# Skewed sums of a delay correlation: both skews read on alternate partitions, halves added by VectorE, one product a tile

## Chip, cores, metric

One NeuronCore of a Trainium2 chip. The time is the device time of one execution in microseconds. Most runs of a kernel agree within 0.3%.

## What is computed

Two layers on x (2 batches, 2048 tokens, width 512): an attention by delays, then a mixture of experts. Only the first matters here:

```python
q, k, v = layernorm(x) @ Wq + bq, ctx @ Wk + bk, ctx @ Wv + bv   # ctx: 128 tokens, padded to L = 2048
qf, kf = rfft(q over time), rfft(k over time)
corr = irfft(qf.real * kf.real + 1j * -(qf.imag * kf.imag), n=L)  # mean over heads and channels
weights, delay = top_k(mean(corr), 15)                            # per batch
out = sum_i softmax(weights)_i * roll(v, delay_i)
x = x + out @ Wo + bo
x = x + shared_expert(layernorm(x)) + routed_experts(layernorm(x))   # 16 experts, 4 a token
```

## The kernel before

Tokens lie in 8 blocks of 512 rows (4 of batch 0, then 4 of batch 1), each of 4 tiles of 128. The engines run hand-written streams that meet by semaphores; each engine's order is the program's.

The kernel needs no FFT. correlate(q) (L704) makes P^T, the product of 128 context rows with a block of 512 normalised tokens, into PSUM, and ScalarE's save_pt (L1163) stores it in `pt[b]`, 128 rows by 2048 columns with 128 columns of wrap-around on either side. The correlation at a delay is a sum over P^T's diagonals. The even part and the odd part of the formula need the sums in both directions. So SyncE writes pt to DRAM (`pt_dram`) and reads it back twice, each row moved by one column more (pitch PTW + 1, `skew_d`) or one less (pitch PTW - 1, `skew_c`): then a diagonal is a column, over 128 partitions. skewed_sum(b, a) (L716) sums the columns of tile a (128 columns, NA = 16 tiles) on TensorE: two products with 32 columns of constants each, of which the last two count: skew_c by (1, 1) and skew_d by (1, -1), which leaves the sum and the difference of the two directions. 16 tiles and 2 batches make 32 sums and 64 products. All are f32, which takes two passes a product.

Batch 0, up to 56 us. skew_early(0) and (1) (columns 0 to 1023, 1024 to 1535) and skew_late(0) (the rest and the wrap) are issued by SyncE as save_pt makes their columns. TensorE weaves the sums into the projections of batch 1's correlation (second_g) and of the values (value_part), L837 to L856. Then come VectorE's save_sums, TensorE's even_parts (three products), VectorE's save_even, TensorE's mean_correlation (17 products), and on VectorE save_mean, best_of_tiles, best_of_all, tile_weights with small DMAs between them, which leave the 15 delays and their weights. SyncE writes these to DRAM and reads them as a circulant tile `st`, with which attention(0) starts. In VectorE's stream moments(6) stands between save_even(0) and save_mean(0). invert_total, x1_tile(0, 0 to 3), x1_moments(0), normalise(7), second_normalise(0), the low halves, x1_tile(1, 0) and vo_low(1) follow attention's start. TensorE waits for vo_low(1) (L896) before it turns the rows of block 0.

GpSimd in this stretch: add_bo(q) adds the output bias to block q of x, four adds of 128 x 512. Five blocks are added from 31 us on, the others after the circulant tile is in and the first weights of the shared expert have been issued. It also issues batch 1's early skewed copies (L2027, L2028), the late ones being SyncE's, and waits for the late ones before it overwrites a buffer beside them.

Batch 1, 100 to 120 us. The shared expert runs in chunks of 128 hidden columns: shared_half(g, half) makes 12 products of 512 columns for gate (half 0) and for up (half 1), ScalarE makes silu(g), VectorE the product, shared_down(g) follows a chunk later. half 0 of chunk g + 1 waits for silu(g) (L996). SUM_AT (L85) says behind which product a sum of batch 1 stands: ten in chunk 0, six in chunk 1. After them even_parts(1) and, behind shared_down(0), mean_correlation(1). logits(1) (L1033) of the router comes at the end of chunk 2, and waits for block 1's turned rows: VectorE normalises, ScalarE and GpSimd split into halves (GpSimd's second_norm_lo, behind its wait for the late skewed copies), SyncE writes them and reads them transposed.

From 130 us on nothing is touched: chunks 2 to 36, 143 blocks of routed experts, the last chunks of the shared expert.

## Time and profile before

| | us |
|---|---|
| median of 3 runs | 997.05 |
| lowest, highest | 996.57, 1002.86 |
| profiled execution | 997.35 |
| its span | 995.5 |

Busy in the span: TensorE 983.8, weight loads (beside the products) 601.3, VectorE 649.9, GpSimd 478.1, ScalarE 380.4. The granted clock of TensorE is at full speed throughout. In a timeline a line is a run of like instructions: start, time from the start of the first to the end of the last, count, and in brackets how long the engine was idle before it and what ended that. Ends of pipelined products overlap the next start, so the time of one is read from start to start. Engines: PE TensorE, DVE VectorE, ACT ScalarE, POOL GpSimd, SPq SyncE's queue.

### The profile page before, as it was taken

How to read it: one execution, taken by the hardware profiler on the slowest of the kernel's cores; microseconds unless marked ns; L12 is line 12 of the kernel's file. 1: busy time of each engine (PE TensorE's matmuls, PEld its weight loads, DVE VectorE, ACT ScalarE, POOL GpSimd, SP SyncE). 2: the span in 40 equal slices, each digit the busy share in tenths (PEclk: the TensorE clock that was granted, in tenths of full speed). 3: DMA queues.
4: the chain of work that ended last, by engine and by line, in shares of the span. 5: the costliest groups of instructions: out<-in, count | busy, mean ns of one | idle time of the engine just before them, and what ended most of it. 6: DMA issues, size and time to landing. Idle time of an engine off the chain costs nothing.

```text
span 995.5 us, 21034 instructions
## 1 busy us (share of the span) xinstructions
PE 983.8 (99%) x6750; PEld 601.3 (60%) x6750; DVE 649.9 (65%) x1506; ACT 380.4 (38%) x776; POOL 478.1 (48%) x540
## 2 busy tenths in 40 slices
PE   8999999999999999999999999999999999999998
PEld 7776644444444445557777777777777544444443
DVE  4977788874488898765555555555455375676765
ACT  3646454443445333324444444444444311111111
POOL 0725412131144577754445444454543376766662
PEclk9999999999999999999999999999999999999999
DMA  9735867868562721558889988889988579999675
GB/s 340 266 126 194 293 196 233 232 184 240 180 180 96 220 66 58 133 140 255 251 240 245 257 236 253 238 252 234 253 253 224 171 237 271 310 259 304 193 225 177
DMA packets 175484, 216.93 MB, mean 218 GB/s; under 512 B 101097, under 2 KB 112233, under 8 KB 174377
## 3 DMA queue, kind: packets, MB, share of 16 engines
q1 hardware_dynamic: 151640, 136.95, 46.6%
q0 software_dynamic: 23760, 78.79, 26.7%
q8 instruction: 61, 1.00, 0.4%
q14 instruction: 23, 0.18, 0.1%
HBM read 123.67 MB, written 69.22 MB: 194 GB/s over the span
## 4 chain that ended last, share of the span: by engine, by line
PE 84%; DVE 7%; DMA 4%; issue 2%; SPq 1%; ACT 1%; POOL 1%; another core or an unknown queue 0%; DVEq 0%; POOLq 0%; ACTq 0%
PE bank L1068 18%; PE bank L941 14%; PE bank L1131 14%; PE bank L1092 9%; PE bank L957 7%; PE bank L1144 7%; PE bank L1051 5%; PE bank L716 2%; PE bank L1082 2%; PE bank L793 1%; DMA arena<-in_x 1%; PE bank L696 1%; SPq L517 1%; PE bank L706 1%; DMA pt_dram<-arena 1%
## 5 line engine op out<-in xcount | busy, mean ns | idle before, releaser
L1068 PE MATMUL bank<-arena 128*128 x1716 | 211.1, 273 | 0.9 <-DVE arena L1608 0.9
L941 PE MATMUL bank<-arena 128*128 128x512 f16 x888 | 202.3, 379 | 0.5 <-DVE arena L1616 0.2
L1068 PEld LDWEIGHTS bank<-arena 128*128 128x128 f16 x1716 | 163.0, 98 | 26.5 <-issue 1.9
L2139 POOL DMA_INDIRECT arena<-y_dram,arena x128 | 137.0, 1071 | 76.8 <-issue 34.2
L2082 POOL DMA_INDIRECT arena<-xr_dram,arena x143 | 139.7, 977 | 58.4 <-issue 47.0
L941 PEld LDWEIGHTS bank<-arena 128*128 128x128 f16 x888 | 87.2, 99 | 101.0 <-DVE arena L1616 0.7
L1131 PE MATMUL bank<-arena 128*128 128x512 f16 x648 | 144.1, 379 | 0.0
L1092 PE MATMUL bank<-arena 128*128 x429 | 115.4, 378 | 0.8 <-ACT arena L1401 0.5
L1884 DVE SCALAR_TENSOR_TENSOR arena<-bank,arena 128x128 f32<-128x128 f32 x143 | 41.7, 292 | 109.7 <-ACT arena L1390 83.6
L1951 DVE SCALAR_TENSOR_TENSOR arena<-arena 128x512 f32<-128x512 f32 x128 | 95.4, 749 | 25.4 <-DMA arena<-y_dram,arena 19.8
L1131 PEld LDWEIGHTS bank<-arena 128*128 128x128 f16 x648 | 63.4, 98 | 76.5
L1338 ACT ACTIVATE arena<-arena 128x512 f16<-128x512 f32 x64 | 40.3, 629 | 171.7 <-DVE arena L1616 94.2
L957 PE MATMUL bank<-arena 128*128 128x512 f16 x444 | 101.9, 379 | 0.3 <-DVE arena L1622 0.3
L1390 ACT ACTIVATE arena<-bank 128x128 f32<-128x128 f32 x143 | 39.7, 278 | 144.4 <-PE bank L1068 92.0
L2075 POOL COPY arena<-arena 128x1 int32 (+1 forms) x143 | 28.1, 197 | 118.9 <-PE bank L1051 109.5
L1401 ACT ACTIVATE arena<-bank 128x512 f32<-128x512 f32 x143 | 83.2, 582 | 1.9 <-PE bank L1092 1.4
L1887 DVE TENSOR_TENSOR arena<-arena 128x128 f16<-128x128 f32 x143 | 41.9, 293 | 53.6 <-ACT arena L1394 49.1
L1608 DVE COPY arena<-bank 128x1024 f16<-128x1024 f16 x108 | 73.7, 682 | 2.9 <-PE bank L1051 1.6
L957 PEld LDWEIGHTS bank<-arena 128*128 128x128 f16 x444 | 43.3, 98 | 52.4 <-DVE arena L1622 0.8
L1144 PE MATMUL bank<-arena 128*128 128x512 f16 x324 | 74.2, 379 | 0.0
L1051 PEld LDWEIGHTS bank<-arena 128*128 128x128 f16 x864 | 57.1, 97 | 26.0 <-DMA arena<-xr_dram,arena 0.9
L2048 POOL TENSOR_TENSOR arena<-arena 128x1024 f32 (+1 forms) x16 | 34.5, 2155 | 69.8 <-ACT arena L1347 58.5
(227 smaller groups left out, 1313.4 us busy)
## 6 DMA issues: line engine op xcount, KB each, us to landing
y_dram<-arena SPq DMA_DIRECT2D x143, 256.0 KB
arena<-in_x SPq DMA_DIRECT2D x8, 1024.0 KB, 12.5
xr_dram<-arena SPq DMA_DIRECT2D x16, 512.0 KB, 4.0
x_dram<-arena SPq DMA_DIRECT2D x8, 1024.0 KB, 5.8
arena<-in_gu_w SPq DMA_DIRECT2D x16, 512.0 KB, 3.5
out<-arena SPq DMA_DIRECT2D x32, 256.0 KB
arena<-x_dram SPq DMA_DIRECT2D x5, 1024.0 KB, 5.9
arena<-in_gu_w POOLq DMA_DIRECT2D x8, 512.0 KB, 4.8
```

Of the source, the lines that this page charges most:

```text
L941: last = mm(bank[half][:, :], (gu_hi_s, gu_lo_s)[wp][:, c, at:at + H], xt[:, xv * KC + kc, :], start=(n == 0), stop=(n == 3 * KC - 1))
L957: last = mm(bank[2 + t][:, :], s_hb[:, g % 2, hv, t * P:t * P + P], (dn_hi_s, dn_lo_s)[wp][:, c, :], start=(c == 0 and n == 0), stop=((c = ...
L1051: last = turn(bank16[p % 2][:, n * P:n * P + P], xg[:, s % 4, n * P:n * P + P], id16)
L1068: last = mm(gate_up_bank(s, s)[:, 0:2 * H], rows[:, xv * KC + kc, :], only((gu_hi_r, gu_lo_r)[wp], e, slice(kc * 2 * H, (kc + 1) * 2 * H)) ...
L1092: last = mm(bank[6 + j][:, :], r_hT[:, j, hv, :], only((dn_hi_r, dn_lo_r)[wp], e), start=(n == 0), stop=(n == 2))
L1131: last = mm(bank[GATE_UP[n % 2][g]][:, :], (gu_hi_s, gu_lo_s)[wp][:, c, at:at + H], xt[:, xv * KC + kc, :], start=(m == 0), stop=(m == 3 * ...
L1144: last = mm(bank[2 + t][:, :], s_hb[:, n % 2, hv, t * P:t * P + P], (dn_hi_s, dn_lo_s)[wp][:, c, :], start=(first and m == 0), stop=(c == ...
L1401: A(y_sb[n % 4], bank[6 + n % 2][:, :], ACT.Copy, scale=1.0 / WS).then_inc(s_ye, 1)
L1608: V.tensor_copy(xgT[:, j, :, :], bank16[j].rearrange("p (n q) -> p n q", n=2 * KC)).then_inc(s_txe, 1)
L1951: V.scalar_tensor_tensor(acc, ybuf[n % RING][:, e, :], w, acc, ALU.mult, ALU.add).then_inc(s_cmb, 1)
L2082: pool.indirect_dma_start(out=dst, out_offset=None, in_=xr_dram[:, :], in_offset=bass.IndirectOffsetOnAxis(ap=token_now[:, r:r + 1], axis= ...
L2139: pool.indirect_dma_start(out=ybuf[n % RING][:, e, :], out_offset=None, in_=y_dram[:, :], in_offset=bass.IndirectOffsetOnAxis(ap=row_of[:, ...
```

## The change

- The two skews are read into one buffer: the one of pitch PTW - 1 on even partitions, the one of pitch PTW + 1 on odd ones. Each partition gets two rows of P^T, r and r + 64, the one in `skew_near`, the other in `skew_far`. In batch 0 one DMA of 64 partitions x 2 rows writes both; in batch 1, where the two buffers are far apart, each copy is two DMAs (GpSimd issues four for two, SyncE six for three).
- VectorE adds far to near (fold_part): columns 128 to 895, 896 to 1407, then (fold_late) 0 to 127 and 1408 to 2047 for batch 0; 128 to 1407, then the rest, for batch 1. `s_fold` counts them, and TensorE waits for it where it waited for the copies.
- A sum is one product, by ones and by +1 on even, -1 on odd partitions.
- TensorE's order for batch 0: second_g(1) without sums, turn_first(4), four sums in each of second_g(2) and (3), value_part(0), the wait for fold 3, the last six sums, value_part(1), even_parts, value_part(2), mean_correlation, value_part(3).
- Batch 1: all 16 sums in chunk 1; fold_part(1) follows x1_moments(1), fold_late(1) stands in VectorE's chunk 0 between the product h and its low half.
- VectorE's splits of the router's weights and its small conversions move from before normalise(5) to behind vo_low(0).
- GpSimd adds three blocks at first, waits until the even parts are saved, adds block 3 and half of block 4, and the other half after the first weights.

Cut to its changed lines:

```diff
@@ -82,8 +82,9 @@
 PACE = (3, 5)
-SUM_AT = {(0, 0, 10): 1, (0, 0, 11): 2, **{(0, 1, n): i + 3 for i, n in enumerate((0, 1, 3, 4, 6, 7, 9, 10))},
-          (1, 0, 11): 0, **{(1, 1, n): n + 11 for n in range(NA - 11)}}
+SUM_AT = {**{(1, 0, n): n + 1 for n in range(10)}, (1, 0, 10): 0, (1, 0, 11): 11,
+          **{(1, 1, n): n + 12 for n in range(NA - 12)}}
+FOLD = P // 2
 WEIGHTS = {1: (3, 4), 2: (5,), 4: (6,), 5: (7,)}
...
@@ -104,7 +105,8 @@
     c[:, C_ID:C_ID + P] = eye
-    c[:, C_ONES:C_ONES + 4] = [1, 1, 1, -1]
+    c[:, C_ONES:C_ONES + 4] = 1
+    c[1::2, C_ONES + 3] = -1
     c[0, C_J0] = 1
...
@@ -174,8 +176,9 @@
         xnT = [view(o + 64 * KB, [KC, BLK]), view(o + 72 * KB, [KC, BLK])]
-        skew_c = [view(o + 80 * KB, [L]), view(o + 88 * KB, [L])]
-        skew_d = [view(o + 88 * KB, [L]), view(24 * KB, [L])]
+        skew_near = [view(o + 80 * KB, [L]), view(o + 88 * KB, [L])]
+        skew_far = [view(o + 88 * KB, [L]), view(24 * KB, [L])]
+        skew_both = view(o + 80 * KB, [2, L])
         xtb_c = view(o + 80 * KB, [2, 2 * KC, BLK], F16)
...
@@ -319,7 +322,11 @@
-            return bass.AP(pt_dram, b * P * PTW + start + first, [[pitch, P], [1, end - first]])
+            return bass.AP(pt_dram, b * P * PTW + start + first, [[pitch, FOLD], [FOLD * pitch, 2], [1, end - first]])
+        def skewed_half(b, start, pitch, first, end, v):
+            return bass.AP(pt_dram, b * P * PTW + start + v * FOLD * pitch + first, [[pitch, FOLD], [1, end - first]])
...
@@ -334,6 +341,7 @@
         s_sk, s_sk2 = ([sem(f"skew_{part}_in{b}") for b in range(B)] for part in ("early", "late"))
+        s_fold = sem("skew_folded")
         s_u, s_u_sb = sem("sums_done"), sem("sums_saved")
...
@@ -460,9 +468,9 @@
                 sp.wait_ge(s_ptw[0], 16 * (n + 1))
-                sp.dma_start(skew_c[0][:, max(lo - M, 0):hi - M], skewed(0, 2 * M - 1, PTW - 1, max(lo - M, 0), hi - M)
-                             ).then_inc(s_sk[0], 16)
-                sp.dma_start(skew_d[0][:, max(lo, M):hi], skewed(0, 1, PTW + 1, max(lo, M), hi)).then_inc(s_sk[0], 16)
+                sp.dma_start(skew_both[0:P:2, :, max(lo - M, 0):hi - M],
+                             skewed(0, 2 * M - 1, PTW - 1, max(lo - M, 0), hi - M)).then_inc(s_sk[0], 16)
+                sp.dma_start(skew_both[1:P:2, :, max(lo, M):hi], skewed(0, 1, PTW + 1, max(lo, M), hi)).then_inc(s_sk[0], 16)
...
@@ -470,9 +478,17 @@
                 sp.wait_ge(s_ptw[b], 16 * (2 if b else len(STEPS[0]) + 2))
-                sp.dma_start(skew_c[b][:, EARLY - M:L], skewed(b, 2 * M - 1, PTW - 1, EARLY - M, L)).then_inc(s_sk2[b], 16)
-                sp.dma_start(skew_d[b][:, EARLY:L], skewed(b, 1, PTW + 1, EARLY, L)).then_inc(s_sk2[b], 16)
-                sp.dma_start(skew_d[b][:, 0:M], skewed(b, 1, PTW + 1, 0, M)).then_inc(s_sk2[b], 16)
+                if b == 0:
+                    sp.dma_start(skew_both[0:P:2, :, EARLY - M:L], skewed(0, 2 * M - 1, PTW - 1, EARLY - M, L)
+                                 ).then_inc(s_sk2[0], 16)
+                    sp.dma_start(skew_both[1:P:2, :, EARLY:L], skewed(0, 1, PTW + 1, EARLY, L)).then_inc(s_sk2[0], 16)
+                    sp.dma_start(skew_both[1:P:2, :, 0:M], skewed(0, 1, PTW + 1, 0, M)).then_inc(s_sk2[0], 16)
+                else:
+                    for v, dst in enumerate((skew_near[1], skew_far[1])):
+                        sp.dma_start(dst[0:P:2, EARLY - M:L], skewed_half(1, 2 * M - 1, PTW - 1, EARLY - M, L, v)
+                                     ).then_inc(s_sk2[1], 16)
+                        sp.dma_start(dst[1:P:2, EARLY:L], skewed_half(1, 1, PTW + 1, EARLY, L, v)).then_inc(s_sk2[1], 16)
+                        sp.dma_start(dst[1:P:2, 0:M], skewed_half(1, 1, PTW + 1, 0, M, v)).then_inc(s_sk2[1], 16)
...
@@ -726,27 +742,20 @@
                 dst = SUMS[b][:, SUM_W * a:SUM_W * a + SUM_W]
-                mm(dst, skew_c[b][:, a * P:a * P + P], c_sb[:, C_ONES + 2 - SUM_W:C_ONES + 2], start=True, stop=False)
-                return mm(dst, skew_d[b][:, a * P:a * P + P], c_sb[:, C_ONES + 4 - SUM_W:C_ONES + 4], start=False, stop=True)
+                return mm(dst, skew_near[b][:, a * P:a * P + P], c_sb[:, C_ONES + 4 - SUM_W:C_ONES + 4],
+                          start=True, stop=True)
...
                     last = mm(dst, lhs(k), rhs(k), start=(k == 0), stop=(k == KC - 1))
-                    if k < len(tiles):
-                        summed = skewed_sum(0, tiles[k])
+                    skewed_sum(0, tiles[k])
                 last.then_inc(s_mm, 1)
-                return summed
...
                                 lambda k: column(kT, k, 1), tiles)
-            def value_part_and_sum(c, tiles):
-                return project_and_sum(bank[5][:, c * M:c * M + M], lambda k: wv_sb[:, k, c * P:c * P + P],
-                                       lambda k: column(ctx_sb, k, 0), tiles)
...
@@ -836,29 +845,30 @@
             second_g(0)
-            pe.wait_ge(s_sk[0], 32)
-            second_g_and_sum(1, (1, 2))
-            skewed_sum(0, 3)
+            second_g(1)
             turn_first(4)
-            for a in (4, 5, 6):
+            pe.wait_ge(s_fold, 1)
+            second_g_and_sum(2, (1, 2, 3, 4))
+            for a in (5, 6):
                 skewed_sum(0, a)
-            pe.wait_ge(s_sk[0], 64)
-            second_g_and_sum(2, (7, 8))
-            second_g_and_sum(3, (9, 10))
+            pe.wait_ge(s_fold, 2)
+            second_g_and_sum(3, (7, 8, 9, 10))
...
             pe.wait_ge(s_pt_sb, 4)
-            pe.wait_ge(s_sk2[0], 48)
-            value_part_and_sum(0, (0, 11, 12))
-            summed = value_part_and_sum(1, (13, 14, 15))
+            value_part(0, bank[5], 0)
+            pe.wait_ge(s_fold, 3)
+            for a in (0, *range(11, NA)):
+                summed = skewed_sum(0, a)
             summed.then_inc(s_u, 1)
-            value_part(0, bank[5], 2)
+            value_part(0, bank[5], 1)
             pe.wait_ge(s_tables, 32)
...
             even_parts(0)
+            value_part(0, bank[5], 2)
+            mean_correlation(0)
             value_part(0, bank[5], 3)
-            mean_correlation(0)
             pe.wait_ge(s_mm_sb, 18)
...
@@ -933,11 +943,11 @@
                     at = kc * 2 * H + half * H
-                    if g == half == 0 and n == 10:
-                        pe.wait_ge(s_sk[1], 32)
+                    if g == 1 and half == 0 and n == 0:
+                        pe.wait_ge(s_fold, 4)
                         pe.wait_ge(s_pt_sb, 7)
-                    if g == 1 and half == 0 and n == 11:
-                        pe.wait_ge(s_sk2[1], 48)
+                    if g == 1 and half == 0 and n == 10:
+                        pe.wait_ge(s_fold, 5)
                     last = mm(bank[half][:, :], (gu_hi_s, gu_lo_s)[wp][:, c, at:at + H], xt[:, xv * KC + kc, :],
...
@@ -1429,6 +1439,17 @@
+            def fold_part(b, lo, hi):
+                near = skew_near[b][:, lo:hi]
+                return V.tensor_tensor(near, near, skew_far[b][:, lo:hi], ALU.add)
+            def fold_late(b):
+                dve.wait_ge(s_sk2[b], 96 if b else 48)
+                fold_part(b, 0, M)
+                fold_part(b, EARLY - M, L).then_inc(s_fold, 1)
             def save_sums(b):
...
@@ -1534,20 +1555,12 @@
             normalise(4)
-            dve.wait_ge(s_misc, 64)
-            dve.wait_ge(s_const, 16)
-            r3 = rt32.rearrange("p (k e) -> p k e", k=KC)
-            link.done(V.tensor_scalar(rt_hi, r3, WS, None, ALU.mult))
-            V.scalar_tensor_tensor(rt_lo, r3, WS, rt_hi, ALU.mult, ALU.subtract).then_inc(s_rt, 1)
-            V.tensor_copy(id16, c_sb[:, C_ID:C_ID + P]).then_inc(s_rt, 1)
-            V.tensor_copy(tri16, cr_sb[:, R_TRI:R_TRI + P])
-            V.memset(chosen_after[:, 0:E], 0.0)
-            V.tensor_copy(places16, cr_sb[:, R_BLK:R_BLK + COLUMNS])
+            for n, (lo, hi) in enumerate(STEPS[0]):
+                dve.wait_ge(s_sk[0], 32 * (n + 1))
+                fold_part(0, max(lo, M) if n == 0 else lo - M, hi - M).then_inc(s_fold, 1)
             V.memset(ones_row[0:1, :], 1.0)
-            dve.wait_ge(s_ids, 1)
-            V.tensor_scalar(token_id, token_int, -ID_MID, None, ALU.add)
-            V.memset(ones16, 1.0).then_inc(s_rt, 1)
             normalise(5)
+            fold_late(0)
             save_sums(0)
...
@@ -1559,6 +1572,18 @@
             vo_low(0)
+            dve.wait_ge(s_misc, 64)
+            dve.wait_ge(s_const, 16)
+            r3 = rt32.rearrange("p (k e) -> p k e", k=KC)
+            link.done(V.tensor_scalar(rt_hi, r3, WS, None, ALU.mult))
+            V.scalar_tensor_tensor(rt_lo, r3, WS, rt_hi, ALU.mult, ALU.subtract).then_inc(s_rt, 1)
+            V.tensor_copy(id16, c_sb[:, C_ID:C_ID + P]).then_inc(s_rt, 1)
+            V.tensor_copy(tri16, cr_sb[:, R_TRI:R_TRI + P])
+            V.memset(chosen_after[:, 0:E], 0.0)
+            V.tensor_copy(places16, cr_sb[:, R_BLK:R_BLK + COLUMNS])
+            dve.wait_ge(s_ids, 1)
+            V.tensor_scalar(token_id, token_int, -ID_MID, None, ALU.add)
+            V.memset(ones16, 1.0).then_inc(s_rt, 1)
...
@@ -1618,6 +1643,8 @@
                     x1_tile(ATTEND[g], 2, 6)
+                if g == 0:
+                    fold_late(1)
                 dve.wait_ge(s_shh, g + 1)
...
@@ -1668,6 +1695,8 @@
             x1_moments(1)
+            dve.wait_ge(s_sk[1], 64)
+            fold_part(1, M, EARLY - M).then_inc(s_fold, 1)
             shared_weights_lo(1)
...
@@ -1992,11 +2021,11 @@
-            def add_bo(q):
+            def add_bo(q, tiles=range(TB)):
...
                 pool.wait_ge(s_xna, 2 * (q + 1))
-                for t in range(TB):
+                for t in tiles:
                     xq = x_sb[:, q * TB + t, :]
...
@@ -2012,27 +2041,33 @@
             pool.wait_ge(s_xn, 2 * 4)
-            for q in range(5):
+            for q in range(HALF - 1):
                 add_bo(q)
+            pool.wait_ge(s_ev_sb, 3)
+            add_bo(3)
+            add_bo(4, (0, 1))
             pool.wait_ge(s_mm, 18)
...
                 shared_weights_in(n)
+            add_bo(4, (2, 3))
             add_bo(5)
...
             pool.wait_ge(s_mm, 28)
-            pool.dma_start(skew_c[1][:, 0:EARLY - M], skewed(1, 2 * M - 1, PTW - 1, 0, EARLY - M)).then_inc(s_sk[1], 16)
-            pool.dma_start(skew_d[1][:, M:EARLY], skewed(1, 1, PTW + 1, M, EARLY)).then_inc(s_sk[1], 16)
+            for v, dst in enumerate((skew_near[1], skew_far[1])):
+                pool.dma_start(dst[0:P:2, 0:EARLY - M], skewed_half(1, 2 * M - 1, PTW - 1, 0, EARLY - M, v)
+                               ).then_inc(s_sk[1], 16)
+                pool.dma_start(dst[1:P:2, M:EARLY], skewed_half(1, 1, PTW + 1, M, EARLY, v)).then_inc(s_sk[1], 16)
             pool.wait_ge(s_wlo, 1)
...
             pool.wait_ge(s_pt, NB)
-            pool.wait_ge(s_sk2[1], 48)
+            pool.wait_ge(s_sk2[1], 96)
             for n in range(4, 6):
...
```

## Rows read from the trace of the kernel before

**Rows 1.** The page's busy line: us, share of the span, instructions.

```profile
PE 983.8 (99%) x6750; PEld 601.3 (60%) x6750; DVE 649.9 (65%) x1506; ACT 380.4 (38%) x776; POOL 478.1 (48%) x540
```

**Rows 2.** Waits of TensorE: us in total, times, longest.

```profile
PE bank L923 <- DMA arena<-xr_dram: 0.3, 1, 0.3
```

**Rows 3.** TensorE's timeline, 47 to 111 us: start us, us, line, [idle before].

```profile
47.12 0.39 PE L729 MATMUL bank<-arena 128*128 128x32 f32 x2
47.34 0.39 PE L730 MATMUL bank<-arena 128*128 128x32 f32 x2
...
56.13 1.06 PE L696 MATMUL bank<-arena 128*128 128x128 f32 x8
...
58.91 3.66 PE L781 MATMUL bank<-arena 128*16 128x128 f32 x32
...
77.59 2.75 PE L793 MATMUL bank<-arena 128*128 128x512 f16 x12 [0.52 <-DMA arena<-g_dram]
...
93.66 0.61 PE L905 MATMUL bank<-arena 128*128 128x128 f16 x8
...
103.03 0.30 PE L729 MATMUL bank<-arena 128*128 128x32 f32 x2
103.17 0.39 PE L730 MATMUL bank<-arena 128*128 128x32 f32 x2
103.39 0.38 PE L941 MATMUL bank<-arena 128*128 128x512 f16 x1
...
110.93 2.75 PE L941 MATMUL bank<-arena 128*128 128x512 f16 x12
```

**Rows 4.** VectorE's timeline, 40 to 93 us.

```profile
40.66 2.97 DVE L1527 TENSOR_SCALAR arena<-arena 128x512 f32<-128x512 f32 x2
...
58.07 2.46 DVE L1509 BATCH_NORM_STATS2 arena<-arena 128x6 f32<-128x512 f32 x4
...
62.61 0.28 DVE L1449 COPY arena<-bank 16x128 f32<-16x128 f32 x1 [1.45 <-PE bank L781]
...
72.48 1.00 DVE L1527 TENSOR_SCALAR arena<-arena 128x512 f32<-128x512 f32 x2
...
78.51 0.75 DVE L1569 SCALAR_TENSOR_TENSOR arena<-bank,arena 128x512 f32<-128x512 f32 x1 [4.35 <-issue]
...
88.62 2.49 DVE L1659 TENSOR_TENSOR arena<-arena 128x512 f16<-128x512 f32 x4
...
92.49 0.67 DVE L1499 TENSOR_TENSOR arena<-bank,arena 128x512 f16<-128x512 f32 x1
```

**Rows 5.** VectorE's timeline, 300 to 308 us, the first beside GpSimd's work.

```profile
300.46 2.50 DVE L1796 TENSOR_TENSOR arena<-arena 128x512 f32<-128x512 f16 x1
...
307.18 0.69 DVE L1796 TENSOR_TENSOR arena<-arena 128x512 f32<-128x512 f16 x1
```

**Rows 6.** GpSimd's timeline, its adds to x.

```profile
30.85 25.31 POOL L2001 TENSOR_TENSOR arena<-arena 128x512 f32<-128x512 f32 x20 [29.87 <-DVE arena L1527]
...
80.46 4.98 POOL L2001 TENSOR_TENSOR arena<-arena 128x512 f32<-128x512 f32 x4
...
96.12 0.56 POOL L2027 DMA_DIRECT2D arena<-pt_dram  x1
```

**Rows 7.** SyncE's queue, two issues at 47 us.

```profile
46.96 0.43 SPq L475 DMA_DIRECT2D arena<-pt_dram  x1
47.43 0.43 SPq L436 DMA_DIRECT2D arena<-in_x  x1
```

**Rows 8.** These two DMAs: KB each, us to landing.

```profile
arena<-pt_dram SPq DMA_DIRECT2D x1, 64.0 KB, 3.3
...
arena<-in_x SPq DMA_DIRECT2D x1, 1024.0 KB, 8.1
```

**Rows 9.** ScalarE's timeline, the first silu.

```profile
109.63 0.60 ACT L1332 ACTIVATE arena<-bank 128x512 f32<-128x512 f32 x1
```

**Rows 10.** Chain that ended last, 76 to 137 us.

```profile
107.72 4.92 DMA arena<-pt_dram
```

## The prediction

> **What bounds the kernel now.** I read the page's busy lines first: TensorE works 983.8 of 995.5 us and every other engine at most two thirds of the span [rows 1]. So time can only be won by taking work from TensorE, and it stays won only if TensorE finds its next inputs ready. Next the waits of TensorE: they are short, and two of them stand in the stretch that the change touches [rows 2, 3]. At 77.59 us it waited 0.5 us for the first circulant tile, the end of the chain mean correlation, best delays, weights, DMA; at 135.8 us it waited 0.3 us for turned rows of block 1. A chain that already ends 0.5 us after TensorE arrives is not shortened by shortening TensorE's filling work; it moves only as far as its own start moves. Last the timeline of each engine from 40 to 136 us, for who would be late once TensorE comes earlier.
>
> **The products removed.** A skewed sum is two f32 products, each in two passes. Back to back one product takes 47.34 - 47.12 = 0.22 us; between the 512-column products of the shared expert a sum takes 103.39 - 103.03 = 0.36 us, of which the first product 0.14 and the second 0.22 [rows 3]. In both places the removed product is worth 0.22 us, so 32 of them are worth 7.1 us, 3.6 us in each batch. This is 0.7% of the time; the two waits could add 0.8 us to it. No more than 8 us can be gained.
>
> **The additions, batch 0.** VectorE adds 128 x 2048 elements in four instructions. A tensor_tensor over 512 columns is 2.49 / 4 = 0.62 us [rows 4], so 768, 512 and 128 + 640 columns are about 0.95, 0.68 and 1.0 us. GpSimd's adds are the disturbance: a VectorE pair that takes 1.00 us alone took 2.97 us beside them, and a tensor_tensor of 0.69 us took 2.50 us [rows 4, 5]. By these rows a VectorE instruction waits until GpSimd's current one (25.31 / 20 = 1.27 us [rows 6]) is over. By the Trainium skill, SBUF — State Buffer, section "Who interferes with whom", a VectorE instruction with two SBUF inputs or in a two-port mode and a GpSimd one exclude each other for a whole instruction; the trace agrees, with the 2.97 us beside 1.00.
>
> GpSimd now stops after 12 adds, at 30.85 + 12 x 1.27 = 46.1 us [rows 6]. The first addition starts when VectorE is through with its pair at 43.5 us [rows 4], waits about 1 us and ends near 45.5 us, when TensorE has its second turned projection and transposes behind it: no wait. The second ends near 46.7 us, before it is asked for. The router's conversions, moved behind VectorE's last work before attention, lie in its idle time there: about 1.4 us in the 4.35 us for which it was idle before its first addition to x at 78.51 us [rows 4]; 1.4 is an estimate, 0.2 us for each of seven small instructions.
>
> The late part is the first that is late. Its last copy is issued at 46.96 us and lands 3.3 us later [rows 7, 8], at 50.3; the addition makes it 51.3 us. When is TensorE there? Before, all sums of batch 0 were done at 56.13 us [rows 3]. Take off 16 x 0.22 = 3.57 us, and what now stands behind the wait: six sums of 0.22 and one value part of 0.9 us (the one at 56.13 us gives way to the even parts 0.9 us later). That is 50.3 us, so TensorE waits about 1.0 us. Bounds: 0 if the copy comes a microsecond early, 2.5 if the new shape of copy costs 1.5 us more.
>
> **The chain to attention.** Before, the mean correlation ended at 58.91 + 3.66 = 62.6 us [rows 3]. Now: 62.6 - 3.57 + 1.0 - 0.9 (one value part placed behind it) = 59.1. But VectorE has moments(6) in front of saving the mean. That block of x is issued at 47.43 and lands 8.1 us later, at 55.5 us [rows 7, 8], so moments(6), which by TensorE's pace could start at 58.07 - 3.57 + 1.0 - 0.9 = 54.6 (the even parts now stand ahead of one more value part), starts at 55.6. It takes 3.1 us (from 58.07 to 61.16, where the idle 1.45 us before 62.61 begins), and its last instruction, a small tensor_scalar, now meets GpSimd's six adds, which begin after the even parts are saved: up to 1 us more, by the pair above; I take 0.8. The mean is saved near 59.5 instead of 62.61 us [rows 4], 3.1 us earlier. From there the chain took 77.59 - 62.61 = 15.0 us; I add 0.5 us, half way between no meeting with GpSimd and one. Attention starts near 75.0 us, 2.6 us earlier. TensorE itself, with the moved value part behind the mean, would be there at 74.5.
>
> **GpSimd's remaining adds.** At 80.46 us GpSimd made four adds in 4.98 us [rows 6]; now it makes six there, 2.5 us more. Counted from the start of attention these fall on VectorE's normalisation of block 7, two tensor_scalars that cost 1.5 instead of 0.5 us each under it, and on two small ones ahead of them: about 2.2 us of delay. VectorE is busy without a gap from there to vo_low(1), which ended at 92.49 + 0.67 = 93.16 us, and TensorE passes the wait for it at 93.66 us [rows 3, 4]. The slack is 0.5 us, so TensorE now waits 2.2 - 0.5 = 1.7 us, taken as 1.6. Bounds: 0 (the VectorE work hides between adds) and 2.5 (all of the GpSimd time). The gain left here is 2.6 - 1.6 = 1.0 us.
>
> **Batch 1.** Chunk 0 loses ten sums of 0.36 us, so TensorE comes to chunk 1 at 110.93 - 3.6 = 107.3 us in the old clock [rows 3]. It may start it only when ScalarE's silu(0) is done, at 109.63 + 0.60 = 110.2 us [rows 9]. ScalarE is not faster; its chain (weights by DMA, conversion, table load, silu) gets 0.3 to 0.5 us longer, because GpSimd issues four copies of 0.56 us instead of two ahead of the weights [rows 6]. So TensorE waits about 3.3 us. In chunk 1 it then makes 16 sums of one product (16 x 0.14 = 2.3 us) where before it made six of two (6 x 0.36 = 2.2 us). Sum: -3.6 + 3.3 + 0.1 = -0.2 us, taken as -0.3. Bounds: -3.5 if silu(0) moves up with TensorE, +1.5 if the weights land as much later as the two more issues last. The 3.6 us of batch 1 are lost almost whole. The late copies of batch 1 are six instead of three, 0.43 us of issue each [rows 7]. Their last landed at 107.72 + 4.92 = 112.6 us [rows 10]; three issues more make it 113.9, less what the writes ahead of them gain, since they now go out before the weights rather than behind them (up to 1.5 us). With 1.0 us for the addition VectorE is done near 114.5; TensorE asks at 110.7 + 10 x 0.36 = 114.3. No wait of size. The rows of block 1 come 0.5 us earlier or later than before; that wait of 0.3 us stays between 0 and 1.
>
> **Sum.** Against the profiled execution's 997.35 us (span 995.5): attention 2.6 earlier, GpSimd's adds -1.6, batch 1 0.3 earlier: 2.6 - 1.6 + 0.3 = 1.3 us earlier in all. 997.35 - 1.3 = 996.05, forecast 996.0. The median of the runs shown, 997.05, is 0.3 us under the profiled one; that is within what runs differ.
>
> **The rivals.**
> - *The gain stays.* If silu(0) and vo_low(1) are no walls because VectorE and ScalarE move up with TensorE, the 7.1 us come through: 990. For it: most of their work is released by TensorE. Against: the idle of ScalarE before silu(0) is a table load and a DMA, and VectorE has no gap before vo_low(1). With one of the two walls only: 992 to 993.
> - *Slower: copies on alternate partitions are slow.* Each now writes 64 partitions two apart. If that doubles their roughly 3 us, the late part of batch 0 lands 2 to 3 us later, TensorE's 1.0 us wait becomes 3 to 4, and batch 1's late part (4.92 us) takes up to 4 more, on the way to chunk 1's tiles and to the rows of block 1: 996 + 2.5 + 4 = 1002.5. It ends above the old time from 1.3 us of extra landing, both batches together. For it: no row has such a pattern. Against: bytes, run lengths and number of runs are the old ones. By the Trainium skill, SBUF — State Buffer, section "Door 1: The DMA port swizzle", the port follows from higher bits of the partition number, so that alternate partitions still reach all of them and nothing is lost; no row here can show it.
> - *Slower by the lock.* If each VectorE instruction of the chain after the mean meets GpSimd, five or so of 1 us, attention does not come earlier: 996 + 2.6 + 1 = 999.5.
> - *The change saves less than it counts.* If a lone product costs 0.22 and not 0.14 between 512-column products, batch 1 costs 16 x 0.08 = 1.3 us more: 997.3.
>
> **How the numbers follow.** Forecast (994 to 998.5, with the last rival in it) 0.60; the gain stays in one or both places (989 to 994) 0.20; slower by the lock (998.5 to 1001) 0.11; slow copies (over 1001) 0.09. The range leaves out some 0.1 on each side: 990.5 to 1001. What a measurement can tell from no change is about 1%, 10 us: faster would need more than the 8 us that there are, 0.02; slower by over 10 us needs slow copies at worse than half rate, 0.04.
>
> **What would show it.** In the profile after: 32 products of 0.22 us gone; TensorE's waits near 50 us (for the addition, 1.0), near 92 us (for VectorE, 1.6) and before chunk 1 (for ScalarE's silu, 3.3); attention starting near 75.0 us; VectorE's normalisation of block 7 at about 1.5 us an instruction. I am wrong if TensorE shows no wait before chunk 1, if the copies land later than 3.3 us after issue, or if attention starts before 74 or after 76.5 us.

## The result, and the profile after

Before 996.57 us (995.94 to 1002.86, 5 runs), after 1007.65 us (1007.05 to 1009.13, 5 runs): ratio 1.0103, 95% interval 1.0084 to 1.0123. The prediction was 996.0, range 990.5 to 1001: the kernel is slower by 1.0%, and the time lies outside the range. The profiled execution took 1009.13 us, 1.5 us more than the median; its span is 1007.3 us, against 995.5 us. Each experiment below has its ratio, with a 95% interval, to the kernel before as it ran beside it on the same chip. There the median of the kernel before lay between 996.98 and 998.99 us, so experiments are compared by their ratios and stages, not by their times.

The page's busy line, where [rows 1] stood for before. The 32 products are gone, at two records each (6750 to 6686), yet TensorE is busy 2.0 us longer:

```profile
PE 985.8 (98%) x6686; PEld 600.9 (60%) x6686; DVE 655.0 (65%) x1513; ACT 380.7 (38%) x776; POOL 475.9 (47%) x542
```

Waits of TensorE after (line, what ended them, us in total, times, longest). Before, the wait for the block's rows was [rows 2], and none stood at the sums:

```profile
PE bank L745 <- DVE arena L1445: 3.9, 1, 3.9
PE bank L802 <- DVE arena L1674: 2.7, 1, 2.7
PE bank L1061 <- DMA arena<-xr_dram,arena: 2.1, 1, 2.1
PE bank L915 <- DVE arena L1520: 1.8, 1, 1.8
```

TensorE's timeline after, answering to [rows 3] (L745 sums, L712 value parts, L780 even parts, L790 mean, L802 attention, also its products woven into the shared expert, L915 turned rows, L951 shared_half):

```profile
49.29 1.14 PE L712 MATMUL bank<-arena 128*128 128x128 f32 x8
54.28 2.77 PE L745 MATMUL bank<-arena 128*128 128x32 f32 x12 [3.85 <-DVE arena L1445]
56.86 2.06 PE L712 MATMUL bank<-arena 128*128 128x128 f32 x8
58.71 0.47 PE L780 MATMUL bank<-arena 128*128 128x32 f32 x2
...
62.24 4.61 PE L790 MATMUL bank<-arena 128*16 128x128 f32 x32
...
82.08 2.75 PE L802 MATMUL bank<-arena 128*128 128x512 f16 x12
...
100.07 0.61 PE L915 MATMUL bank<-arena 128*128 128x128 f16 x8 [1.76 <-DVE arena L1520]
...
116.02 1.46 PE L802 MATMUL bank<-arena 128*128 128x512 f16 x3 [2.66 <-DVE arena L1674]
118.52 0.61 PE L951 MATMUL bank<-arena 128*128 128x512 f16 x1 [1.03 <-ACT arena L1342]
```

A value part takes 2.06 us instead of 1.06, the mean 4.61 instead of 3.66 [rows 3]. The busy time by stretches after says why (the columns are the length of the stretch, the busy time of TensorE, weight loads, VectorE, ScalarE and GpSimd, then the granted clock, DMA share, GB/s):

```profile
50.00:52.00 2.00, 0.43 (x4) 0.24 (x3) 0.00 (x0) 0.13 (x1) 0.00 (x0) 1.00 0.81 201
52.00:54.00 2.00, 0.00 (x0) 0.00 (x0) 0.80 (x2) 0.00 (x0) 0.00 (x0) 0.98 1.06 398
54.00:64.00 10.00, 9.72 (x45) 8.86 (x46) 4.44 (x16) 0.00 (x0) 3.51 (x3) 0.50 0.58 214
...
116.00:122.00 6.00, 4.94 (x19) 3.32 (x20) 5.24 (x10) 4.98 (x7) 1.08 (x2) 0.50 0.87 279
```

The granted clock was 1.00 (2.4 GHz) until the wait, and 0.50 (1.2 GHz) for the 10 us behind it; the same again from 116 us, behind the wait before chunk 1. Where the copies went, in SyncE's queue after ([rows 7, 8] before), first the three late copies as issued, then their landings, then the first addition in VectorE's timeline:

```profile
46.93 0.59 SPq L482 DMA_DIRECT2D arena<-pt_dram  x1
47.56 0.61 SPq L484 DMA_DIRECT2D arena<-pt_dram  x1
48.22 0.61 SPq L485 DMA_DIRECT2D arena<-pt_dram  x1
```

```profile
arena<-pt_dram SPq DMA_DIRECT2D x1, 320.0 KB, 3.3
arena<-pt_dram SPq DMA_DIRECT2D x1, 256.0 KB, 3.2
arena<-pt_dram SPq DMA_DIRECT2D x1, 64.0 KB, 5.0
```

```profile
53.20 1.03 DVE L1445 TENSOR_TENSOR arena<-arena 128x128 f32<-128x128 f32 x2 [5.05 <-DMA arena<-pt_dram]
```

The last copy is issued 1.3 us later than before and takes 5.0 instead of 3.3 us: 53.2 instead of 50.3 us, and the addition starts at that moment. TensorE came to its wait at 54.28 - 3.85 = 50.43 us.

Start of the stages in each profiled execution, us (late sums: TensorE's last six sums of batch 0; mean: its mean correlation; attention, turned rows: of block 0; even(1): the even parts of batch 1; entry: the first turned rows of the routed experts; the rest is the span behind it):

| kernel | late sums | mean | attention | turned rows | chunk 0 | even(1) | entry | rest |
|---|---|---|---|---|---|---|---|---|
| before | with the value parts | 58.91 | 77.59 | 93.66 | 100.64 | 119.19 | 430.14 | 565.4 |
| after | 54.28 | 62.24 | 82.08 | 100.07 | 107.23 | 128.38 | 439.18 | 568.1 |
| a1_plain_copies | 50.84 | 54.96 | 73.93 | 92.05 | 99.21 | 120.87 | 431.18 | 567.7 |
| a2_keep_clock | 54.60 | 58.82 | 77.71 | 95.75 | 102.90 | 124.12 | 435.33 | 573.3 |
| a3_batch0_only | 53.23 | 61.19 | 80.97 | 98.92 | 106.08 | 125.83 | 436.48 | 567.5 |
| a4_batch1_only | as in before | 59.06 | 77.80 | 93.86 | 100.85 | 120.89 | 431.65 | 568.0 |
| b1_halves | 54.73 | 62.68 | 82.09 | 100.04 | 107.20 | 130.33 | 440.85 | 566.8 |
| b2_no_pause | 54.25 | 62.20 | 81.39 | 97.46 | 104.44 | 126.21 | 436.71 | 569.3 |
| b3_fill | 53.01 | 56.55 | 77.12 | 95.22 | 102.39 | 124.63 | 435.48 | 567.3 |
| b4_silu_first | as in before | 58.47 | 77.36 | 93.42 | 100.41 | 127.76 | 438.01 | 569.1 |
| c1_batch0_filled | 54.37 | 58.73 | 79.53 | 95.60 | 102.59 | 121.59 | 431.85 | 564.7 |
| c2_before_again | as in before | 58.88 | 77.64 | 93.70 | 100.69 | 120.31 | 431.07 | 564.8 |
| c3_batch1_clock | as in before | 58.54 | 77.29 | 93.35 | 100.34 | 122.53 | 432.80 | 564.7 |
| d1_batch0_covered | 56.27 | 60.39 | 79.49 | 95.56 | 102.54 | 122.03 | 433.05 | 564.9 |

Of the 11.8 us of span lost, 4.5 are there at attention, 1.9 more at the turned rows, 2.8 more at even(1), and 2.8 behind the entry. How much one trace can be trusted is seen from before and c2_before_again, which are the same kernel: they differ by 1.1 us at even(1), where only the second waits 1.15 us for batch 1's early copies, and by 0.9 us at the entry. A difference of about 1 us between two single traces is therefore not shown to come from an edit.

### The profile page after: what moved, and what is told of

Same layout as the page of the kernel before. It is cut to its first block, busy times and chain, and to the rows that moved or that the text cites. A ratio compares the mean times of both kernels' runs of the same rounds, so it can differ in the third digit from the quotient of the medians.

```text
span 1007.3 us, 20919 instructions
## 1 busy us (share of the span) xinstructions
PE 985.8 (98%) x6686; PEld 600.9 (60%) x6686; DVE 655.0 (65%) x1513; ACT 380.7 (38%) x776; POOL 475.9 (47%) x542
## 4 chain that ended last, share of the span: by engine, by line
PE 80%; DVE 9%; DMA 5%; issue 3%; SPq 2%; ACT 1%; POOL 1%; DVEq 0%; POOLq 0%; ACTq 0%
PE bank L1078 18%; PE bank L1141 14%; PE bank L951 13%; PE bank L1102 9%; PE bank L967 7%; PE bank L1154 6%; PE bank L1061 5%; PE bank L732 2%; PE bank L1092 2%; DMA pt_dram<-arena 1%; DMA arena<-in_x 1%; DVE arena L1884 1%; DMA arena<-pt_dram 1%; SPq L533 1%; PE bank L802 1%
## 5 line engine op out<-in xcount | busy, mean ns | idle before, releaser
L951 PE MATMUL bank<-arena 128*128 128x512 f16 x888 | 203.3, 380 | 1.7 <-ACT arena L1342 1.0
L951 PEld LDWEIGHTS bank<-arena 128*128 128x128 f16 x888 | 88.0, 100 | 103.3 <-ACT arena L1342 1.9
L1061 PE MATMUL bank<-arena 128*128 128x128 f16 x864 | 66.2, 219 | 2.9 <-DMA arena<-xr_dram,arena 2.1
```

The source lines that it names most:

```text
L951: last = mm(bank[half][:, :], (gu_hi_s, gu_lo_s)[wp][:, c, at:at + H], xt[:, xv * KC + kc, :], start=(n == 0), stop=(n == 3 * KC - 1))
L1061: last = turn(bank16[p % 2][:, n * P:n * P + P], xg[:, s % 4, n * P:n * P + P], id16)
```

## The experiments

**The form of the copies.** a1_plain_copies keeps all else of after, but copies as before (all 128 partitions, one row each); it leaves out the split into even and odd partitions that the constants count on, so its sums are not the right ones:

```diff
-sp.dma_start(skew_both[0:P:2, :, EARLY - M:L], skewed(...))   # pitch PTW - 1
-sp.dma_start(skew_both[1:P:2, :, EARLY:L], skewed(...))       # pitch PTW + 1
+sp.dma_start(skew_near[b][:, EARLY - M:L], skewed_all(...))   # and so for all copies
+sp.dma_start(skew_far[b][:, EARLY:L], skewed_all(...))
```

> The changed kernel with its skewed copies in the old form: each skew read by one DMA into all 128 partitions, one row each, in both batches and from both issuing engines. VectorE still adds two buffers, TensorE still makes one product a tile (the sums are then not those of the reference). Theory 'copies': the new form is what comes late (issues of 0.60 us for 0.43, the last late copy landing at 53.2 for 50.3 us), so here the last addition of batch 0 ends near 51.5 us, TensorE waits about 1 us before it instead of 3.9, its clock stays at full speed from 54 to 64 us, attention starts near 76 us instead of 82, the time is 1000 to 1002. Theory 'order': the wait comes from TensorE being early and from the additions, whatever the copies; then it stays at 3 us or more, the clock falls, and the time stays within 2 us of 1007.65.

Measured: 1001.29 us, ratio 1.0018 (0.9996 to 1.0039). The last late copy in its SyncE queue:

```profile
46.58 0.43 SPq L487 DMA_DIRECT2D arena<-pt_dram  x1
```

It landed after 3.0 us. TensorE's timeline and clock of a1_plain_copies:

```profile
50.84 1.42 PE L741 MATMUL bank<-arena 128*128 128x32 f32 x12
...
110.30 0.61 PE L947 MATMUL bank<-arena 128*128 128x512 f16 x1 [3.20 <-ACT arena L1338]
```

```profile
50.00:66.00 16.00, 16.00 (x112) 12.61 (x112) 11.57 (x37) 6.24 (x19) 7.40 (x6) 1.00 0.51 188
106.00:110.00 4.00, 0.82 (x3) 0.21 (x3) 3.91 (x8) 3.22 (x4) 1.09 (x2) 0.83 0.55 159
110.00:115.00 5.00, 4.70 (x21) 4.08 (x22) 2.99 (x7) 2.67 (x4) 1.41 (x3) 0.50 0.96 325
```

No wait, no slow clock in batch 0, attention 8.15 us earlier than in after and 3.7 earlier than before: between these two traces the form of the copies costs 8.0 us up to the entry. But at even(1) it is 1.7 us behind before (0.6 behind c2_before_again): TensorE's waits for VectorE (1.9 us before the turned rows, 0.94 us before chunk 1) and for silu (3.20 us) with a slow clock behind them take the 3.7 us.

The landing of the last late copy varies from trace to trace. In the six profiled executions with the plain form in batch 0 it landed at 49.6 to 51.2 us, 3.0 to 4.4 us after its issue; in the seven with the alternate form at 51.9 to 53.5 us, 4.0 to 5.0 us after it. So the form makes it later in every trace, but by 1.6 us between the middle values; after, with 53.2 us, is one of the two latest.

**The clock's share.** a2_keep_clock is after with products of zeros into an unused bank in the wait:

```diff
+            pe.wait_ge(s_mm_sb, 14)
+            for _ in range(4):
+                mm(bank[7][:, :], zeros[:, 0:P], zeros, start=True, stop=True)
             pe.wait_ge(s_fold, 3)
```

> The changed kernel with four products of 512 columns of zeros (0.86 us each at full clock) on TensorE just before its wait for the third addition of batch 0. They fill 3.4 of the 3.9 us of that wait and change nothing else. Theory 'clock': half of what the wait costs is the clock that falls behind it (0.50 from 54 to 64 us); then the granted clock is 1.00 there, attention starts 4 to 5 us earlier than in the changed kernel (near 77.5 us for 82.1), the time is 1002 to 1004. Theory 'chain alone': attention hangs on the landing copies and on VectorE, not on TensorE's clock; then attention and the time move by under 1 us.

The clock in a2_keep_clock:

```profile
52.00:66.00 14.00, 13.93 (x89) 10.00 (x88) 8.26 (x26) 2.81 (x7) 7.37 (x6) 1.00 0.58 222
```

The sums stand as late as in after (54.60 us), attention starts 4.4 us earlier. So the 8.15 us between a1 and after are 3.8 of later copies (a2 against a1, in the sums' start 3.76 and at attention 3.78) and 4.4 of clock. The time did not follow: 1012.3 us, 1.0105 (1.0041 to 1.0169), where 1002 to 1004 us was expected. At the entry 3.85 us were left of it; the rest, 573.3 us, is the longest of all kernels, from waits that I can't tie to the edit. The clock's 4.4 us are thus shown at attention and up to the entry, and not in the whole time.

**Which half of the kernel.** a3_batch0_only has batch 1 and SUM_AT as before, a4_batch1_only batch 0 and GpSimd's adds as before:

```diff
# a3
-SUM_AT = {**{(1, 0, n): n + 1 for n in range(10)}, (1, 0, 10): 0, (1, 0, 11): 11, ...
+SUM_AT = {(0, 0, 10): 1, (0, 0, 11): 2, **{(0, 1, n): i + 3 ...
# a4
-pe.wait_ge(s_fold, 2)
-second_g_and_sum(3, (7, 8, 9, 10))
+second_g_and_sum(2, (7, 8))
+second_g_and_sum(3, (9, 10))
```

> The change in batch 0 alone, with GpSimd's pause and the moved conversions; batch 1 has the copies, two products a sum, and places in chunks 0 and 1 of the kernel before. By the stages of the changed trace (attention 4.5 us later, the rows of block 0 another 1.9, even parts of batch 1 another 2.8, entry to the experts another 2.8) batch 0 carries 6.4 us: 1003 to 1005 if the loss at the experts' entry is a matter of batch 1 or of chance, 1006 if it goes with any delay. Rival: batch 1 carries most of the loss by its DMAs; then this is under 1001.

> The change in batch 1 alone: batch 0, VectorE's conversions and GpSimd's adds as in the kernel before; batch 1 with copies on alternate partitions (four and six), one product a sum, all sums in chunk 1, additions on VectorE. By the stages it carries 2.8 us up to the even parts of batch 1, with TensorE's waits before chunk 1 (for VectorE's low weights and ScalarE's first silu) and a clock at 0.5 behind them: 999 to 1001. If the waits before chunk 1 come from VectorE being late out of batch 0 they vanish, and it is 995 to 998.

Measured: a3 1005.86 us, 1.0067 (1.0037 to 1.0097); a4 1001.38 us, 1.001 (0.9987 to 1.0032). Batch 0 carries the loss, 6.3 us at the entry against before and 5.4 against c2_before_again. Batch 1 alone is 1.5 or 0.6 us later there, and its ratio can't be told from 1. It gains nothing either, though its chunk 0 is 3.6 us shorter: TensorE's waits of 2.00 us for silu and 0.77 for VectorE, and the clock at 0.50 from 112 to 114 us behind them, take that.

**Step or halving.** b1_halves puts the one skew on partitions 0 to 63, the other on 64 to 127:

```diff
-sp.dma_start(skew_both[0:P:2, ...
+sp.dma_start(skew_both[0:FOLD, ...
-sp.dma_start(skew_both[1:P:2, ...
+sp.dma_start(skew_both[FOLD:P, ...
```

> The changed kernel with the two skews on halves of the partitions (the one on 0 to 63, the other on 64 to 127) instead of on alternate ones, and the -1 of the constants on the upper half; rows a partition, number of DMAs, additions and order stay. The plain form issued in 0.43 us and its last late copy of batch 0 landed at 49.6 us; the alternate form issued in 0.60 us and landed at 53.2. Theory 'stride': the step of two partitions is what slows the copies; then they issue in 0.43 us here, land near 50 us, TensorE's wait for the third addition is 0 to 1.5 us and attention starts at 74 to 76. Theory 'half': a DMA that fills only 64 partitions is slower (by the Trainium skill, SBUF — State Buffer, section on the DMA port swizzle, 64 neighbouring partitions reach half the ports and get half the rate, alternate ones all); then the copies land as late as the alternate ones or later, at 53 us or more, and attention starts at 82 or later.

Measured: 1012.7 us, 1.0147 (1.0118 to 1.0176). Issue and landings of the late copies in b1_halves:

```profile
49.64 0.61 SPq L485 DMA_DIRECT2D arena<-pt_dram  x1
```

```profile
arena<-pt_dram SPq DMA_DIRECT2D x1, 320.0 KB, 3.9
arena<-pt_dram SPq DMA_DIRECT2D x1, 256.0 KB, 4.2
arena<-pt_dram SPq DMA_DIRECT2D x1, 64.0 KB, 4.0
```

The issue of these three costs 0.58 to 0.61 us here too, against 0.32 to 0.43 of the same three in before: it doesn't come from the step of two. Nor does it come from the two rows: batch 1's late copies in after take 64 partitions by one row, and cost SyncE 0.53 to 0.60 us each. What remains common is the 64 partitions. Part of it falls on neighbours: in after the x block behind the three copies, whose form is unchanged, took 0.60 us of issue instead of 0.43.

In landing there is a difference. The two large late copies land 3.9 and 4.2 us after issue, against 3.2 to 3.5 in all seven traces with alternate partitions; the first two copies of all, 448 KB each, after 4.8 and 5.9 us against 3.8 to 4.4. The small last one, 4.0 us, lies among the 4.0 to 5.0 of the others. It landed at 53.6 us, and attention came at 82.09, as the theory 'half' had it. The Trainium skill, SBUF — State Buffer, section "Door 1: The DMA port swizzle", has 64 neighbouring partitions reach half the ports, and by its formula alternate ones reach all; the slower landings agree with it in direction.

**GpSimd's pause.** b2_no_pause adds five blocks first, as before:

```diff
-for q in range(HALF - 1): add_bo(q)
-pool.wait_ge(s_ev_sb, 3)
-add_bo(3); add_bo(4, (0, 1))     # and add_bo(4, (2, 3)) later
+for q in range(5): add_bo(q)
```

> The changed kernel with GpSimd's adds placed as before: twenty from 31 us on without a pause, four behind the first weights. Theory 'the pause only moves the harm': the first additions and the normalisation of block 5 get some 3 us slower, in time in which VectorE was idle for 5 us, the third addition ends within 1.3 us of where it did (54.2), and TensorE's wait of 1.8 us before the rows of block 0 (VectorE's 2.9 us for a small instruction beside six adds) goes; time 0.5 to 2 us under the changed kernel. Rival, the pause is needed: the third addition comes over 2 us later, and the time is 2 us or more over the changed kernel.

Measured: 1008.79 us, 1.0101 (1.0064 to 1.0138). TensorE no longer waits before the turned rows (they come 16.07 us behind attention, as before, instead of 17.99) and the entry is 2.5 us earlier; the ratio, 1.0101 for 1.0103 of after, doesn't show it, and decides for neither theory. The pause did save something as well: without it the third addition takes 2.09 instead of 1.03 us beside GpSimd's adds, which is why the sums start no earlier (54.25 us), although the copies landed 1.2 us sooner than in after. What the wait is made of, VectorE and GpSimd of after:

```profile
89.40 2.88 DVE L1607 TENSOR_SCALAR arena<-arena 128x4 f32<-128x4 f32 x1
...
92.48 1.00 DVE L1548 TENSOR_SCALAR arena<-arena 128x512 f32<-128x512 f32 x2
```

```profile
84.83 7.41 POOL L2030 TENSOR_TENSOR arena<-arena 128x512 f32<-128x512 f32 x6
```

One instruction of four columns takes 2.88 us, until the last of GpSimd's six adds is over (84.83 + 7.41 = 92.24); behind it the normalisation runs at its usual 0.5 us each. The same instruction took 2.83 to 3.00 us in all six traces with the pause, and 0.55 to 0.57 us in the eight without it.

**Real work in the wait.** b3_fill is after with all four value parts ahead of the wait; c1_batch0_filled is the same on a3, with no pause:

```diff
-            value_part(0, bank[5], 0)
+            for c in range(KC):
+                value_part(0, bank[5], c)
             pe.wait_ge(s_fold, 3)
```

> The changed kernel with the other three value parts of batch 0 (0.9 us each) placed before TensorE's wait for the third addition instead of behind it. The wait falls from 3.9 to about 1.1 us. Theory 'clock': with that the granted clock stays at 1.00, and the mean correlation ends near 61 us for 66.8, attention starts near 76.3 for 82.1, and the rows of block 0 follow near 94; the time is 1001 to 1003. If attention moves by only 2.7 us (the work moved), the clock was not part of the loss.

> The change in batch 0 alone, with two of its losses taken out: all four value parts stand before TensorE's wait for the third addition, and GpSimd adds as before, without a pause. By the stages: attention near 76.5 to 77.2 us (77.6 before, 77.1 with the filled wait), the rows of block 0 at 16.1 us behind it (the distance before, and without the pause), so 93.0 us for 93.7. Theory 'copies bound it': what is left of the 3.6 us is under 1 us, since the sums cannot start before the last copy and addition; time within 1.5 us of the kernel before on the same chip, 0.5 us under it at best. Rival: something beyond these two costs time as well (the longer issues in SyncE's queue, x blocks that land later); then it is 2 us or more over.

> The kernel before, for its stages on this chip. On the first chip the first turned rows of the experts began at 430.1 us and 565.4 us followed; in the changed kernels 567 to 573 us followed. If the part behind the experts' entry, which no kernel here changes, is longer by the chip or by chance, it is 567 us or more here too. If it is 565 to 566 us, the later loss belongs to the change.

Measured: b3 1007.1 us, 1.0079 (1.0055 to 1.0103); c1 1000.68 us, 1.0033 (1.0023 to 1.0044); c2, which is before once more, 997.78 us in its one run. TensorE's timeline and clock in c1_batch0_filled (L748 sums, L785 even parts, L793 and L795 mean):

```profile
54.37 1.53 PE L748 MATMUL bank<-arena 128*128 128x32 f32 x12 [0.96 <-DVE arena L1448]
56.44 0.61 PE L785 MATMUL bank<-arena 128*128 128x32 f32 x2 [0.54 <-DVE arena L1461]
...
58.73 5.61 PE L795 MATMUL bank<-arena 128*16 128x128 f32 x32
```

```profile
56.00:62.00 6.00, 5.13 (x24) 3.95 (x25) 3.56 (x15) 0.67 (x2) 1.87 (x2) 0.50 0.59 221
```

The wait is down from 3.85 to 0.96 us and the clock still falls, behind that and a gap of 0.54 us for VectorE's copies of the sums; the mean takes 5.61 instead of 3.66 us. In b3_fill TensorE doesn't wait for the addition at all (sums at 53.01 us), and what it did before the clock fell are two small gaps with 32-column products around them:

```profile
55.07 0.38 PE L780 MATMUL bank<-arena 128*128 128x32 f32 x2 [0.54 <-DVE arena L1456]
...
56.32 0.39 PE L788 MATMUL bank<-arena 128*16 128x128 f32 x2 [0.43 <-DVE arena L1462]
```

```profile
56.00:58.00 2.00, 1.68 (x13) 1.39 (x14) 2.00 (x7) 0.00 (x0) 1.66 (x2) 0.84 0.94 345
58.00:60.00 2.00, 2.00 (x11) 1.43 (x10) 1.93 (x7) 0.00 (x0) 2.00 (x2) 0.50 0.46 174
```

The value parts that after and before put between these steps cover such gaps; b3 and c1 had taken them away.

Against what was expected: b3's attention came at 77.12 us, 5.0 us earlier than in after, where 76.3 was named for the theory 'clock'; but the clock did not stay at 1.00, and the time missed the 1001 to 1003 us. c1's attention came at 79.53 us, not at 76.5 to 77.2, and it is 3.7 us over the kernel before, as its rival had it (2 us or more): what it had left out is the clock, and the third addition, which takes 2.29 us beside GpSimd's adds. c2's rest is 564.8 us, by which the later loss would belong to the change. But c1 and c3, with one half of the change each, have 564.7 on the same chip; so neither half alone shows it there.

**Batch 1's walls.** b4_silu_first is a4 with ScalarE's and VectorE's conversion of chunk 2's weights moved behind silu(0); c3_batch1_clock is a4 with twelve unused products behind logits(0):

```diff
# b4
-            second_std(1); shared_weights_hi(2)
+            second_std(1)                        # shared_weights_hi(2) behind save_logits(0)
# c3
                     logits(0, xtb_c[:, 0, :, :])
+                    for _ in range(12):
+                        mm(bank[3][:, :], gu_hi_s[:, 0, 0:P], xtb_c[:, 0, 0, :], start=True, stop=True)
```

> Batch 1's part of the change alone, with the conversion of the third chunk of shared weights (ScalarE's high half, VectorE's low half) moved from before chunk 0's silu to behind its logits. In batch 1 alone TensorE waited 0.8 us for VectorE's and 2.0 us for ScalarE's work before chunk 1, with the clock at 0.50 from 112 to 115 us. Theory 'silu is the wall': the silu no longer stands behind those weights' landing, the wait before chunk 1 falls under 1 us, the clock stays, and the even parts of batch 1 come at 118 to 119 us instead of 120.9; time 1 to 2.5 us under batch 1 alone. Rival 'late copies are the wall': TensorE then waits as long a little later, at the product of tile 0, for the last addition (fold 5), and the even parts come at 120.5 or later.

> Batch 1's part of the change alone, with twelve products of 512 columns (2.6 us) on TensorE behind the first logits, into a bank that is overwritten later. They fill most of the 2.8 us for which it waits before chunk 1, so that the clock stays at 1.00 where it was 0.50 from 112 to 115 us. Theory 'clock': the 3.5 us at half clock cost some 1.4 us, and the even parts of batch 1 come at 119.5 us for 120.9. Theory 'late copies': the product of tile 0 then waits that long for the last addition, which ended at 115.6 us; the even parts stay at 120.5 to 121.

Measured: b4 1008.61 us, 1.0097 (1.007 to 1.0123); c3 998.68 us, 1.0016 (1.0006 to 1.0025). TensorE's waits in chunk 1 of b4_silu_first:

```profile
115.27 0.61 PE L963 MATMUL bank<-arena 128*128 128x512 f16 x1 [3.49 <-DVE arena L1457]
...
122.49 1.46 PE L815 MATMUL bank<-arena 128*128 128x512 f16 x3 [5.65 <-DVE arena L1602]
```

and of c3_batch1_clock:

```profile
110.82 0.39 PE L963 MATMUL bank<-arena 128*128 128x512 f16 x1 [1.09 <-ACT arena L1356]
115.65 0.39 PE L963 MATMUL bank<-arena 128*128 128x512 f16 x1 [1.09 <-DVE arena L1459]
117.05 1.21 PE L815 MATMUL bank<-arena 128*128 128x512 f16 x3 [0.51 <-DVE arena L1604]
```

In b4 the wait for silu is gone. The first long wait that took its place, 3.49 us, is the one that the rival 'late copies' named: it stands at the product before tile 0 and is for the last addition, for which VectorE itself sat idle for 4.26 us until the last copy landed at 114.2 us. The second, 5.65 us, is of the edit's own making: VectorE's conversion (L1682), moved behind the addition, took 4.77 us, until the end of a GpSimd addition of 128 x 2048 (117.14 + 4.07 = 121.21 us). even(1) comes 6.9 us later than in a4, so the edit gains nothing; but it shows that behind silu the late copies are the next wall.

c3 shows the same wall: TensorE comes to the late addition 1.09 us too early. The clock, 1.00 up to 116 us, then falls behind this wait and the one of 0.51 us:

```profile
118.00:120.00 2.00, 2.00 (x10) 1.68 (x9) 1.45 (x2) 0.00 (x0) 2.00 (x1) 0.50 0.73 277
```

So the cover moved the slow clock and didn't remove it, and even(1) comes at 122.53 us, 1.6 us later than in a4 and later than either theory named. In a4 the slow clock hides the wall: TensorE comes to the addition at 115.8 us, which ended at 115.6.

**Both covered.** d1_batch0_covered is c1 with two value parts and six products of zeros ahead of the wait, and the other two value parts in the small gaps:

```diff
             value_part(0, bank[5], 0); value_part(0, bank[5], 1)
+            for _ in range(6): mm(bank[7][:, :], zeros[:, 0:P], zeros, start=True, stop=True)
             pe.wait_ge(s_fold, 3)               # then sums, value part 2, even parts, value part 3, mean
```

> Change in batch 0 alone, as in c1_batch0_filled (batch 1's copies and sums as before, GpSimd's adds as before), with every small gap covered: value parts 0 and 1 and six products of zeros (128x512, about 0.43 us each, left in as cover) ahead of the wait for the addition, value part 2 between the sums and the even parts, value part 3 between the even parts and the mean. Theory (the copies set when the sums are done; the rest of the loss in batch 0 is TensorE's clock): no wait of over 0.3 us from 49 to 62 us, granted clock 1.00 there, last six sums at about 54.3, the mean ends near 62.0 us instead of c1's 64.34, attention starts near 77.0 (before: 77.59, c1: 79.53); logits(0) near 110.0; at the end 0.5 us less than before, so a ratio of 0.998 to 1.002 and no measurable gain: the form gains nothing in batch 0 even with its waits covered. Rival (the clock falls at this place from other causes than TensorE's gaps): clock 0.50 at 56 to 62 us again, attention at 79 or later, ratio 1.003 as c1. A gain of over 2 us would say that the later landing isn't the wall.

Measured: 999.59 us, 1.0039 (1.002 to 1.0058). TensorE in d1_batch0_covered, and its clock in two of the stretches between 52 and 64 us, all of which are at 1.00:

```profile
51.12 5.32 PE L869 MATMUL bank<-arena 128*128 128x512 f32 x12
56.27 1.42 PE L748 MATMUL bank<-arena 128*128 128x32 f32 x12
...
79.49 2.75 PE L807 MATMUL bank<-arena 128*128 128x512 f16 x12 [0.95 <-DMA arena<-g_dram]
```

```profile
56.00:58.00 2.00, 2.00 (x18) 1.76 (x17) 0.27 (x3) 0.00 (x0) 1.60 (x2) 1.00 0.96 345
58.00:60.00 2.00, 2.00 (x20) 2.00 (x19) 0.79 (x5) 0.00 (x0) 0.00 (x0) 1.00 0.50 188
```

The rival is out: without gaps the clock stays. The ratio is above the 0.998 to 1.002 that I expected, so d1 is no better than c1 (1.0033); its attention, 79.49 us, isn't either. The attention I named (77.0) was missed because a 512-column f32 product takes (56.27 - 51.12) / 6 = 0.86 us in two records, and the 0.43 that I wrote is one record: the cover ended near 56.3 us, 1.9 us after c1's sums could start. Taking 1.9 off leaves attention at an estimated 77.6 us, where before has 77.59; that version was worked out, not run. Nor was one that lets GpSimd pause for the third addition alone (2.10 us here, 1.03 with the pause) and still spreads its later adds; by these numbers it could bring another 1.1 us at attention. No kernel run here beats the one before.

## Why the prediction was wrong, by its steps

Between the profiled executions the forecast was 1.3 us less span, and 11.8 us more were measured: it is off by 13.1 us. By its terms: attention 2.6 earlier forecast, 4.5 later measured, 7.1 off; GpSimd's adds 1.6 forecast, 1.9 measured; batch 1 up to even(1) 0.3 earlier forecast, 2.8 later measured, 3.1 off; behind the entry 0 forecast, 2.8 measured. A slip without weight in it: 16 x 0.22 us is 3.52, not the 3.57 taken off.

- **The late part of batch 0: wrong, and this carries the result.** The step took 0.43 us of issue and 3.3 us of landing from [rows 7, 8] for copies of another form, and made the last one land at 50.3 us with a wait of 1.0 us, bounds 0 to 2.5. It landed at 53.2 us and the wait was 3.85. TensorE's side of the step was right: 50.3 us forecast for its arrival, 50.43 measured. Of the 2.9 us, 0.8 are the write of P^T ahead of the copies, which was issued no later but landed after 3.4 instead of 2.6 us, and held back the first of them; 0.4 are the two issues before the last one, at 0.2 more each; 1.7 are the landing. a1 confirms that the form of the copies is the cause: with the old form and all else of after the write lands after 2.0 us, there is no wait, and attention comes at 73.93 us, 1.1 before the forecast. Why the form costs issue and landing is not shown.
- **TensorE's clock: missing.** No term of the sum held it; the page before showed it at full speed, and I priced the wait by its length alone. Behind 3.85 us of idling TensorE ran at 0.50 for 10 us, worth 4.4 us at attention by a2, more than the rest of the miss there. The Trainium skill, TensorE: Matmul & The Clock Gate, section "HAM oscillation — how this bites in real kernels", has DMA waits drop the array to half rate so that the next products run slowly; the rows agree.
- **The rival.** "Copies on alternate partitions are slow" was the right direction, at a chance of 0.09, but not the right sizes. It doubled the landing; measured are 3.1 to 3.3, 3.0 to 3.2 and 3.3 to 5.0 us for the three late copies of batch 0, and the slower issues and the write that it didn't have. It gave 1002.5 us; with the clock's 4.4 that would be 1006.9, near the 1007.65 by luck, since 4 of it stand for batch 1's late copies, and a4, which has these, is at most 1.5 us later at the entry. I had set the chance by bytes and ports, and these don't tell the issue: it is slower on alternate partitions and, in b1, just as much on neighbouring ones.
- **The chain behind the even parts.** 15.0 us forecast from the mean's end to attention with 0.5 added; measured 82.08 - 66.85 = 15.2. Right. The small instruction of moments(6) was to take 0.8 us more beside GpSimd's adds and did, 0.99 instead of 0.17.
- **GpSimd's remaining adds.** Wait of 1.6 us forecast, 1.76 measured, by another way: not slower normalisation (1.5 us each forecast, 0.5 measured) but one four-column instruction held for 2.88 us. The size was right and the way was not, so its closeness is in part luck. b2 shows that the adds are the cause.
- **Batch 1.** 3.3 us before chunk 1 forecast, 2.66 + 1.03 = 3.7 measured, the larger part for VectorE instead of ScalarE; in a4, where batch 0 is not late, they are 0.77 and 2.00, the larger part for ScalarE as forecast. Two things lacked: the slow clock at 116 to 122 us, and the late addition, called "no wait of size", for which TensorE waits 1.09 us in c3 and 3.49 in b4. Net -0.3 forecast; a4 shows +1.5 at the entry against one trace of the kernel before and +0.6 against the other.
- **The routed experts.** Nothing was forecast there. TensorE waits 2.1 us for gathered rows in after, its clock is at 0.50 from 454 to 456 us behind that, and the rest is 2.8 us longer than before's. In the other kernels that rest lies between 564.7 and 573.3 us, and not by the edits: c3 has a4's change and 564.7 us where a4 has 568.0. The profiled execution of after is also the slowest of its five, 1.5 us over their median. These 2.8 us stay open.

## What to carry to other kernels

Price a DMA by a row of the same access form, and where there is none, take the issue and the landing as unknown and let the chance of the slow case be large. A wait that is new in a TensorE stream can cost its length and then the clock: here 3.85 us brought 4.4 more, and in b3 the clock fell behind no more than two gaps of 0.54 and 0.43 us. Products laid into every gap held the clock (a2, d1), value parts in one block ahead of the wait did not (b3, c1); but where a landing sets the end, products saved ahead of it gained nothing in d1 even then. Before a difference of 1 us between two traces is given to an edit, a second trace of the same kernel is worth its time: here it took away most of batch 1's loss.

## What the runs showed of the hardware that I had not expected

- SyncE's issue of a copy into 64 partitions took mostly 0.58 to 0.61 us with two rows each, with the step of two or without (0.71 to 0.74 for the first of all), and 0.53 to 0.60 us with one row (batch 1 of after). The same bytes into 128 partitions by one row took 0.32 to 0.43 us in 38 of 42 issues and 0.58 to 0.75 in the other four. GpSimd's issues took 0.52 to 0.56 us in either form.
- The granted clock fell to 0.50 behind idle times of 0.54 and 0.43 us in b3; it stayed at 1.00 in d1, which has none there.
- A VectorE instruction of 128 x 4 took 2.88 us beside six GpSimd adds in a row, to the end of the last, and not only to the end of the one in progress; without them it took 0.55 to 0.57 us. In b4 one of 128 x 512 took 4.77 us beside one GpSimd addition of 128 x 2048.
